# The post chain of an attention and expert kernel: Newton steps, scale and shift on GpSimd, stores of the query and key parts on SyncE's queue

## The chip, the cores and the metric

The kernel runs on one core of a Trainium2 chip. The metric is the device time in microseconds of one execution. The kernel before takes 821.72 us, the median of three runs (817.86 to 822.37). Engines: PE (TensorE, matmuls), DVE (VectorE), ACT (ScalarE), POOL (GpSimd), and SP (SyncE), which here only issues DMAs. Each takes its own instructions in order, and they wait for each other by semaphores.

## The reference

Batch 4, sequence 1024, width 128, 16 heads of width 8. All in float32.

```python
mod = (silu(c) @ wmod).reshape(4, 6, 1, 128)        # sa, ca, ga, sb, cb, gb
h = layernorm(x) * (1 + ca) + sa
Q, K, V = heads(h @ Wq.T + bq), heads(h @ Wk.T + bk), heads(h @ Wv.T + bv)
scores = Q @ K.T / sqrt(8) + lam * (tanh(Q) @ J) @ tanh(K).T     # causal
x = x + ga * ((softmax(scores) @ V) @ Wo.T + bo)
h = layernorm(x) * (1 + cb) + sb
expert = argmax(h @ centroids.T)                    # one of 8 for each row
y = h + relu((layernorm(h) * gamma + beta) @ W1.T + b1) @ W2.T + b2  # of that expert
x = x + gb * (alpha * y + (1 - alpha) * h)          # alpha = sigmoid(h . centroid)
```

## The kernel before

The work on a batch has three parts. *Preparation*: layer norm, the projections Q, K, V and the product with J, and the split of q, tanh k, k and J's product into three bf16 parts each, which go to HBM (`q_parts`, `k_parts`) and come back as stacks for the matmuls. *Attention*: four groups of four heads, g0 to g3. *The post chain*: the attended values are divided by their denominators, projected (O0, O1), added to x, normalised, scaled and shifted (this is h), multiplied with the centroids (S), the experts are chosen and counted (C), h is normalised again, and the rows of the payload are scattered to a table sorted by expert (`by_expert`). The post chain of the last batch runs in the tail, beside the experts' matmuls on 46 tiles.

A body of the main program runs the attention of batch b, the preparation of b+1 (in g0) and the post chain of b-1. The bodies are "first" (b = 0), "middle" (b = 1 and 2, a loop) and "last" (b = 3). In a group, PE makes 48 score blocks (12 units of 4 heads); ACT takes the exponential of each, PE multiplies it with the values two units later. Between the score blocks stand "items". Most of them are chunks of raw scores for the group after ("m"), whose row maxima DVE takes out of four PSUM banks. The last chunk is followed on DVE by four short steps that split the maxima into three parts (`mparts`, lines 1640 to 1643), PE turns them (item T), DVE copies them (`mrow`), and SP sends them with four DMAs (line 431, `send_maxima`) into the stacks of the next group, which can't begin before.

A table sets where in a group the items of the post chain stand: `POST_AT` for the middle body, `POST_LAST` for the last. A number there is a place out of 33 in the group's list of items. A planner (`schedule`) then lays the list over the 48 slots of PE by costs for DVE and PE. In the kernel before it puts in the middle body `attended` at slot 4 of g2, O0 at slot 10, O1 at 14, the 15 steps of the first inverse square root (`root_x`, by Newton's method, on 128x8 values) at slots 17 to 27, `scale_h` and `shift_h` at 36 and 38, H0 and H1 (transposes of h) at 43, S at the end; g3 has `best`, the 15 steps of `root_h`, C at 20 and `place`. The last body has the same in g1 and g2.

SP issues in a fixed order (`attention` in the SP block): outputs of each half group (`store_half`, line 436), the maxima, the reciprocal denominators `r_den` (`store_reciprocals`, 480), then `load_outputs` (495, 496): NUM and DEN, which `attended` multiplies. These lie where Q and K of the next batch lay until all parts were stored. The stacks of the next batch follow (`load_group`, 414). POOL splits the four tensors (631 to 636), issues three stores after each (677), then adds the residual's bias (669), and later makes the payload (688 to 700) and scatters it (712).

## Time and profile before

| | us |
|---|---|
| median of three runs | 821.72 |
| profiled execution | 825.38 |
| span of its instructions | 823.7 |
| busy: PE | 697.3 |
| busy: DVE | 569.8 |
| busy: ACT | 499.5 |
| busy: POOL | 232.3 |

The profiled execution is one run with the hardware profiler; its span is from its first to its last instruction. Busy times are sums over the whole span and say nothing of which engine ends a wait at a given place. Work of the post chain is seen in the stretches 300.6 to 389.9 (batch 0's chain), 466 to 553 (batch 1's) and 583.4 to 662.1 (batch 2's). The attention ends at 688.6. In the rows, `arenaB` holds NUM, DEN, the product AT, h and the payload, `ln` and `stat` the small values of the norms.

### The profile page before, as it was taken

How to read it: one execution, taken by the hardware profiler on the slowest of the kernel's cores; microseconds unless marked ns; L12 is line 12 of the kernel's file. 1: busy time of each engine (PE TensorE's matmuls, PEld its weight loads, DVE VectorE, ACT ScalarE, POOL GpSimd, SP SyncE). 2: the span in 40 equal slices, each digit the busy share in tenths (PEclk: the TensorE clock that was granted, in tenths of full speed). 3: DMA queues.
4: the chain of work that ended last, by engine and by line, in shares of the span. 5: the costliest groups of instructions: out<-in, count | busy, mean ns of one | idle time of the engine just before them, and what ended most of it. 6: DMA issues, size and time to landing. Idle time of an engine off the chain costs nothing.

```text
span 823.7 us, 17084 instructions
## 1 busy us (share of the span) xinstructions
PE 697.3 (85%) x5087; PEld 349.8 (42%) x5087; DVE 569.8 (69%) x1408; ACT 499.5 (61%) x1182; POOL 232.3 (28%) x218
## 2 busy tenths in 40 slices
PE   4666899999999988898899888999989879898694
PEld 2352334334334333333333334333424225788594
DVE  6959677888757777686577776778886712587453
ACT  1440786675687754575877645667575668566482
POOL 2028039400004920203049202030001400355643
PEclk9776899999999998899999998899999989998998
DMA  8995824293261349063504480537303244432520
GB/s 225 312 178 209 138 48 117 67 184 74 49 113 33 115 116 169 3 109 108 90 24 124 108 177 2 98 108 147 121 14 117 91 158 131 129 106 87 195 61 13
DMA packets 52563, 92.04 MB, mean 112 GB/s; under 512 B 10305, under 2 KB 26205, under 8 KB 51960
## 3 DMA queue, kind: packets, MB, share of 16 engines
q1 hardware_dynamic: 43404, 70.28, 36.1%
q0 software_dynamic: 6400, 17.86, 6.9%
q10 hardware_dynamic: 2668, 2.78, 1.3%
q8 instruction: 46, 0.75, 0.4%
q14 instruction: 45, 0.37, 0.2%
HBM read 51.04 MB, written 37.90 MB: 108 GB/s over the span
## 4 chain that ended last, share of the span: by engine, by line
PE 47%; DVE 19%; issue 11%; ACT 8%; DMA 8%; SPq 3%; POOL 1%; ACTq 1%; DVEq 1%; POOLq 0%
PE PS L1173 12%; PE PS L1199 10%; PE PS L1133 10%; DVE PS L1621 5%; ACT arenaA L956 5%; PE PS L1250 4%; PE PS L1261 3%; SPq L431 3%; DVE arenaB L1296 2%; DMA arenaB<-r_den 2%; DVE block_max L1628 2%; PE PS L1203 2%; DMA arenaA<-mrow 2%; ACT arenaB L874 2%; PE PS L1082 1%
## 5 line engine op out<-in xcount | busy, mean ns | idle before, releaser
L956 ACT ACTIVATE arenaA<-PS 128x512 f32<-128x512 f32 (+3 forms) x768 | 330.8, 497 | 199.4 <-PE PS L1203 157.5
L1621 DVE CUSTOM_DVE_ANT_0 PS<-PS,mask 128x1024 f32<-128x1024 f32 (+3 forms) x256 | 261.5, 1036 | 98.7 <-PE PS L1133 91.4
L1199 PE MATMUL PS<-arenaA 99*128 99x512 bf16 (+3 forms) x768 | 223.6, 337 | 23.8 <-ACT arenaA L956 9.3
L1133 PE MATMUL PS<-arenaA 96*128 96x512 bf16 (+3 forms) x768 | 202.3, 340 | 32.6 <-DVE maxima L1621 15.6
L1199 PEld LDWEIGHTS PS<-arenaA 99*128 99x128 bf16 x768 | 72.6, 98 | 220.4 <-ACT arenaA L956 132.2
L1173 PE MATMUL PS<-arenaA,Vs 128*9 128x512 f32 (+3 forms) x1536 | 163.8, 503 | 0.0
L1628 DVE TENSOR_REDUCE block_max<-PS 128x8 f32<-128x1024 f32 (+1 forms) x96 | 100.2, 1044 | 24.4 <-PE PS L1138 23.4
L1133 PEld LDWEIGHTS PS<-arenaA 96*128 96x128 bf16 x768 | 66.7, 101 | 99.8 <-DVE maxima L1621 42.0
L1203 PE MATMUL PS<-after,identb 128*128 128x128 bf16 x512 | 107.0, 225 | 1.1 <-issue 1.1
L631 POOL TENSOR_TENSOR arenaB<-arenaB 128x1024 f32<-128x1024 f32 x12 | 25.7, 2144 | 180.1 <-ACT arenaB L810 180.0
L1005 ACT ACTIVATE arenaA<-PS,b1p 128x128 f32<-128x128 f32 x184 | 52.7, 373 | 35.2 <-PE PS L1250 35.2
L768 POOL DMA_INDIRECT out_dram<-arenaA x46 | 45.8, 996 | 92.8 <-DVE arenaA L1296 90.4
L1250 PE MATMUL PS<-arenaA 128*128 128x128 f32 x368 | 53.0, 290 | 7.4 <-DVE arenaA L1752 7.3
L1203 PEld LDWEIGHTS PS<-after,identb 128*128 128x128 bf16 x512 | 51.5, 101 | 5.5 <-issue 2.0
L688 POOL TENSOR_TENSOR arenaB<-arenaB,MB 128x1024 f32<-128x1024 f32 x3 | 7.1, 2360 | 163.1 <-DVE arenaB L1296 163.1
L1261 PE MATMUL PS<-arenaA 128*128 x368 | 50.9, 284 | 1.9 <-issue 1.9
L1250 PEld LDWEIGHTS PS<-arenaA 128*128 128x128 f32 x368 | 47.7, 203 | 10.5 <-DVE arenaA L1752 10.4
L1138 PE MATMUL PS<-identb,after 128*128 128x128 bf16 x256 | 51.2, 228 | 0.0
L1261 PEld LDWEIGHTS PS<-arenaA 128*128 128x128 f32 x368 | 46.9, 200 | 2.5 <-issue 2.4
L1173 PEld LDWEIGHTS PS<-arenaA,Vs 128*9 128x9 f32 x1536 | 23.7, 89 | 51.9 <-ACT arenaA L956 26.6
L1621 DVE DVE_READ_ACCUMULATOR2_ANT maxima<- 128x1 f32 x256 | 36.1, 141 | 0.0
L1752 DVE COPY arenaA<-PS 128x128 f32<-128x128 f32 x46 | 12.9, 282 | 33.3 <-PE PS L1241 33.1
(195 smaller groups left out, 718.3 us busy)
## 6 DMA issues: line engine op xcount, KB each, us to landing
arenaA<-k_parts SPq DMA_DIRECT2D x96, 128.0 KB, 7.7
arenaA<-by_expert SPq DMA_DIRECT2D x46, 192.5 KB, 3.6
o_raw<-OT SPq DMA_DIRECT2D x32, 256.0 KB, 2.3
arenaA<-q_parts SPq DMA_DIRECT2D x16, 384.0 KB, 4.9
q_parts<-arenaB POOLq DMA_DIRECT2D x18, 256.0 KB, 3.8
k_parts<-arenaB POOLq DMA_DIRECT2D x18, 256.0 KB, 3.8
arenaA<-in_L_ffn_W_dram SPq DMA_DIRECT2D x2, 2048.0 KB, 13.3
arenaA<-q_parts SPq DMA_DIRECT2D x16, 256.0 KB, 5.7
```

The costliest lines, as they stand in the source:

```text
L768: g.indirect_dma_start(out_rows, bass.IndirectOffsetOnAxis(ap=XSI[n % NX][:, 3 * D:3 * D + 1], axis=0), YS[:, n % U, :], None, bounds_chec ...
L956: a.activation(PT[:, u % EB, h, off:HALF], PS[:, 4 + n % SB_, off:HALF], ACT.Exp).then_inc(exp_ok, 1)
L1005: last = a.activation(HR[:, n % 3, k * P:(k + 1) * P], PS[:, 3 + n % 2, k * P:(k + 1) * P], ACT.Relu, bias=b1p[:, bass.ds(expert[n] * FC + ...
L1133: last = mm(PS[:, place + c0 // HALF, at:at + c1 - c0], SQ(g, h)[0:KROWS, t * P:(t + 1) * P], SK(g, h)[0:KROWS, c0:c1], start=(at == 0), s ...
L1138: last = mm(diag, after[:, :], identb[:, :], start=False, stop=True, skip_group_check=True)
L1173: last = mm(PS[32 * h:32 * h + VW, 7, off:HALF], Vs[:, g, (kb * HG + h) * VW:(kb * HG + h + 1) * VW], PT[:, u % EB, h, off:HALF], start=(k ...
L1199: last = mm(bank[:, off:HALF], SK(g, h)[0:MROWS, kb * P:(kb + 1) * P], SQ(g, h)[0:MROWS, qc * HALF + off:(qc + 1) * HALF], start=True, sto ...
L1203: last = mm(bank[:, off:off + P], identb[:, :], after[:, :], start=False, stop=True, skip_group_check=True)
L1250: last = mm(PS[:, 3 + n % 2, k * P:(k + 1) * P], W1C[n % 3][:, k * P:(k + 1) * P], XT[:, n % 3, :], start=(k == 0), stop=True, skip_group_ ...
L1261: last = mm(PS[:, 6 + n % 2, 0:D], HR[:, n % 3, k * P:(k + 1) * P], W2T[:, bass.ds(expert[n] * FF + k * P, P)], start=(k == 0), stop=(k == ...
L1621: v.tensor_tensor_reduce(out=src, in0=src, in1=mask[:, S - n:S], scale=1.0, scalar=-3e38, op0=ALU.add, op1=ALU.max, accum_out=maxima[:, pl ...
L1628: v.tensor_reduce(block_max[:, place % 2, heads[0]:heads[-1] + 1, t, 0:t + 1], src.rearrange("p h (c q) -> p h c q", q=P), AX.X, ALU.max). ...
```

## The change

The post chain starts one group earlier: in the middle body `attended`, O0, O1 and the statistics of x stand in g1, H0, H1, S and the choice of the expert in g2, C and the places in g3. In the last body `attended` to the statistics of x stand in g0, with the reciprocals moved there from place 18 to 12, and the rest in g1 and g2. By the planner's list, in the middle body `attended` is at slot 24 of g1, O0 at 30, O1 at 33, the second half of the statistics at 37, H0 at slot 27 of g2, H1 at 28, S at 33, C at slot 4 of g3. In the last body the reciprocals are at slot 18 of g0 and `attended` at 35.

The steps of both inverse square roots for batches 0 to 2 go from DVE to POOL (`pool_moment`, 22 instructions in 18 steps that wait for each other), as do scale and shift. ACT's norms wait for them at fixed units (`NORMS_AT`). The first guess of the root takes one instruction fewer, and so has every chain 14 steps on DVE, in the tail too.

POOL no longer issues the stores of the parts. It adds the residual's bias first and then makes the four splits. SP issues the stores (`store_parts`) at four places of its order, and loads NUM and DEN between the third and the fourth tensor, as soon as the splits of Q and K are made.

```diff
         POST = ("O0", "O1", "H0", "H1", "S", "C")
         LEAD = -1400
         NEWTON = 3
-        MOMENTS = 6 + 3 * NEWTON
-        root = lambda name, n0, at, n1=MOMENTS: tuple((at + (n - n0) // 2, "D", (name, n)) for n in range(n0, n1))
-        ATT = 4
-
+        MOMENTS, POOL_MOMENTS = 5 + 3 * NEWTON, 6 + 4 * NEWTON
         POST_AT = {0: ((24, "D", "denominators"),),
-                   2: ((ATT, "D", "attended"), (ATT + 2, "R", "O0"), (ATT + 3, "D", "stats_x0"), (ATT + 4, "R", "O1"),
-                       (ATT + 5, "D", "stats_x1")) + root("root_x", 0, ATT + 6) +
-                      ((ATT + 14, "D", "bias_x"), (ATT + 19, "D", "scale_h"), (ATT + 20, "D", "shift_h"),
-                       (ATT + 22, "R", "H0"), (ATT + 23, "R", "H1"), (ATT + 23, "D", "stats_h0"), (ATT + 25, "D", "stats_h1"), (ATT + 27, "R", "S")),
-                   3: tuple(it for n in range(6) for it in ((n, "D", ("best", n)), (n, "D", ("root_h", 2 * n)), (n, "D", ("root_h", 2 * n + 1)))) +
-                      root("root_h", 12, 6) + ((8, "D", "bias_h"), (8, "D", "weigh"), (9, "R", "C")) +
-                      tuple((11 + n, "D", ("place", n)) for n in range(3))}
-
-        POST_LAST = {0: ((18, "D", "denominators"),), 1: POST_AT[2], 2: POST_AT[3] + ((15, "D", "pads"),), 3: ((0, "D", "table"),)}
+                   1: ((17, "D", "attended"), (19, "R", "O0"), (20, "D", "stats_x0"), (21, "R", "O1"), (23, "D", "stats_x1")),
+                   2: ((18, "R", "H0"), (19, "R", "H1"), (19, "D", "stats_h0"), (20, "D", "stats_h1"), (21, "R", "S")) +
+                      tuple((23 + n, "D", ("best", n)) for n in range(6)) + ((29, "D", "weigh"),),
+                   3: ((2, "R", "C"),) + tuple((4 + n, "D", ("place", n)) for n in range(3))}
+        NORMS_AT = dict(middle=dict(x=(2, 2), h=(3, 1)), last=dict(x=(1, 2), h=(2, 1)))
+
+        POST_LAST = {0: ((12, "D", "denominators"), (24, "D", "attended"), (26, "R", "O0"), (27, "D", "stats_x0"), (28, "R", "O1"),
+                         (29, "D", "stats_x1")),
+                     1: POST_AT[2], 2: POST_AT[3] + ((9, "D", "pads"),), 3: ((0, "D", "table"),)}
...
-        BEST_IN = dict(middle=3, last=2)
+        BEST_IN = dict(middle=2, last=1)
...
+        POS0_NUM, POS0_DEN = [next(n for n, it in enumerate(TENSORS) if it[0] == k) for k in (0, 1)]
...
+            def store_parts(b, n):
+
+                k, dst, off = TENSORS[n]
+                sp.wait_ge(split_ok, b * 4 + n - 3)
+                sp.sem_inc(sp_turn, 1)
+                for j in range(3):
+                    sp.dma_start(dst[bass.ds(b, 1), :, j, off:off + HD, :].rearrange("a h r q -> (a h) r q"),
+                                 T16[:, k, j, :]).then_inc(parts_out, 16)
+
             def prepared(b):
 
-                sp.wait_ge(stored, b + 1)
-                sp.sem_inc(sp_turn, 1)
+                sp.wait_ge(parts_out, b * PARTS_OUT)
+                sp.sem_inc(stored, 1)
...
-                    sp.wait_ge(stored, b + 3)
+                    sp.wait_ge(split_ok, b * 4 + 4 + POS0_NUM + 1)
                     sp.sem_inc(sp_turn, 1)
                 if not last:
                     sp.dma_start(NUM[:, :], by_head(b)[:, 0:HD, :]).then_inc(num_in, 16)
+                if not isinstance(b, int):
+                    sp.wait_ge(split_ok, b * 4 + 4 + POS0_DEN + 1)
+                    sp.sem_inc(sp_turn, 1)
                 sp.dma_start(DEN[:, :], r_den[bass.ds(b, 1), :, :].rearrange("a h (o q) -> (a h) o q", o=1).to_broadcast([H, HD, S]))\
                     .then_inc(num_in, 16)
 
...
                 if body != "first":
                     load_denominators(b - 1)
                 for g in range(NG):
+                    if body != "last" and g == 1:
+                        store_parts(b + 1, 2)
+                        if body == "middle":
+                            load_outputs(b - 1)
+                        store_parts(b + 1, 3)
                     store_half(b, g, 0)
...
-                    if g == 1 and body == "middle":
-                        load_outputs(b - 1)
                     if body == "last" and g == 2:
                         begin(0)
+                    if body != "last" and g == 0:
+                        store_parts(b + 1, 0)
                     store_half(b, g, 1)
...
+                    if g == 0 and body != "last":
+                        store_parts(b + 1, 1)
...
             def split_batch(b):
-                for n, (k, dst, off) in enumerate(TENSORS):
+                residual(b)
+                for n in range(len(TENSORS)):
                     split(b, n, split_ok)
-                    pool.wait_ge(split_ok, b * 4 + n - 3)
+
+            L2 = lambda k: ln2[:, k, :]
+
+            def pool_moment(n):
+
+                L, y = lambda k: ln2[:, k, :], ln2[:, 7, :]
+                if n == 0:
+                    g.tensor_tensor(L(0), stat2[:, :, 1], stat2[:, :, 4], ALU.add)
+                    g.tensor_tensor(L(2), stat2[:, :, 2], stat2[:, :, 5], ALU.add)
+                    return g.tensor_tensor(L(1), stat2[:, :, 1], stat2[:, :, 4], ALU.subtract)
+                if n == 1:
+                    g.tensor_scalar(L(0), L(0), -0.5, None, ALU.mult)
+                    g.tensor_scalar(L(2), L(2), 1.0 / D, EPS, ALU.mult, ALU.add)
+                    return g.tensor_scalar(L(1), L(1), 0.5, None, ALU.mult)
+                if n == 2:
+                    return g.tensor_tensor(L(3), L(1), L(1), ALU.mult)
+                if n == 3:
+                    return g.tensor_tensor(L(5), L(3), L(2), ALU.add)
+                if n == 4:
+                    return g.tensor_scalar(y.bitcast(I32), L(5).bitcast(I32), -0.5, float(0x5f3759df), ALU.mult, ALU.add)
+                if n == POOL_MOMENTS - 1:
+                    return g.tensor_tensor(L(8), L(0), y, ALU.mult)
+                if n % 4 == 1:
+                    return g.tensor_tensor(L(6), y, y, ALU.mult)
+                if n % 4 == 2:
+                    return g.tensor_tensor(L(6), L(6), L(5), ALU.mult)
+                if n % 4 == 3:
+                    return g.tensor_scalar(L(6), L(6), -0.5, 1.5, ALU.mult, ALU.add)
+                return g.tensor_tensor(y, y, L(6), ALU.mult)
+
+            def moments(b, which, stats_ok, moments_ok):
+
+                pool.wait_ge(stats_ok, b + 1)
+                pool.sem_inc(pool_turn, 1)
+                for n in range(POOL_MOMENTS):
+                    ins = pool_moment(n)
+                    if n == POOL_MOMENTS - 1:
+                        ins.then_inc(moments_ok, 1)
+                        return
+                    ins.then_inc(moments_step, 1)
+                    pool.wait_ge(moments_step, (b * 2 + which) * (POOL_MOMENTS - 1) + n + 1)
                     pool.sem_inc(pool_turn, 1)
-                    for j in range(3):
-                        pool.dma_start(dst[bass.ds(b, 1), :, j, off:off + HD, :].rearrange("a h r q -> (a h) r q"),
-                                       T16[:, k, j, :]).then_inc(parts_out, 16)
-                residual(b)
-                pool.wait_ge(parts_out, b * PARTS_OUT)
-                pool.sem_inc(stored, 1)
+
+            def scale_shift(b):
+
+                over = lambda k: MB[:, bass.ds(b, 1), k, :].to_broadcast([P, TB, D])
+                pool.wait_ge(x_normed, b + 1)
+                pool.sem_inc(pool_turn, 1)
+                g.tensor_tensor(H2, H2, over(2), ALU.mult).then_inc(h_scaled, 1)
+                pool.wait_ge(h_scaled, b + 1)
+                pool.sem_inc(pool_turn, 1)
+                g.tensor_tensor(H2, H2, over(1), ALU.add).then_inc(h2_ok, 1)
 
             def row_sums(b):
                 over = lambda k: MB[:, bass.ds(b, 1), k, :].to_broadcast([P, TB, D])
+                pool.wait_ge(stored, min(b + 3, B) if isinstance(b, int) else b + 3)
+                pool.sem_inc(pool_turn, 1)
                 pool.wait_ge(h2_ok, b + 1)
                 pool.sem_inc(pool_turn, 1)
                 g.tensor_tensor(PAY[:, :, D:2 * D], H2, over(3), ALU.mult).then_inc(pool_step, 1)
+                moments(b, 1, h_stats, h_moments)
                 pool.wait_ge(pool_step, b * 4 + 1)
...
             def send_rows(b):
 
+                moments(b, 0, x_stats, x_moments)
+                scale_shift(b)
                 row_sums(b)
...
-            def post_norm(b, dst, src, first, count):
-
-                act.wait_ge(post_chain, b * LINKS + count)
+            def post_norm(b, dst, src, first, moments_ok):
+
+                act.wait_ge(moments_ok, b + 1)
...
-                    for name, g, which in (("bias_x", BEST_IN[body] - 1, (norm_x0, norm_x1)), ("bias_h", BEST_IN[body], (norm_h0, norm_h1))):
-                        u = unit_of(body, g, "D", name)
+                    for name, which in (("x", (norm_x0, norm_x1)), ("h", (norm_h0, norm_h1))):
+                        g, u = NORMS_AT[body][name]
                         for n, step in enumerate(which):
-                            steps.setdefault((g, min(NU - 1, u + n)), []).append((1 + n, step, -1))
+                            steps.setdefault((g, u + n), []).append((1 + n, step, -1))
...
-                    return v.tensor_scalar(L(6).bitcast(I32), L(5).bitcast(I32), 1, None, ALU.logical_shift_right)
-                if n == 5:
-                    return v.tensor_scalar(L(7).bitcast(I32), L(6).bitcast(I32), -1.0, float(0x5f3759df), ALU.mult, ALU.add)
+                    return v.tensor_scalar(L(7).bitcast(I32), L(5).bitcast(I32), -0.5, float(0x5f3759df), ALU.mult, ALU.add)
+                if n % 3 == 2:
+                    return v.scalar_tensor_tensor(L(6), L(7), -0.5, L(7), ALU.mult, ALU.mult)
                 if n % 3 == 0:
-                    return v.scalar_tensor_tensor(L(6), L(7), -0.5, L(7), ALU.mult, ALU.mult)
-                if n % 3 == 1:
                     return tt(L(6), L(6), L(5), ALU.mult)
                 return v.scalar_tensor_tensor(L(7), L(6), 1.5, L(7), ALU.add, ALU.mult)
...
-                    last.then_inc(post_chain, 1)
+                    last.then_inc(post_chain if isinstance(b, int) and b == B - 1 else done, 1)
...
-                elif step in ("bias_x", "bias_h"):
-                    linked(b, AT_NORM_X if step == "bias_x" else AT_NORM_H)
-                    v.scalar_tensor_tensor(L2(8), L2(0), -1.0, L2(7), ALU.mult, ALU.mult).then_inc(post_chain, 1)
```

The semaphores of the new steps are added too, and `row_sums` waits for the stores before it writes the payload over the parts.

DVE in the last body. The first piece is of before, in g0, where the reciprocals stand (DENP is their tile; `ISA PS,maxima` is the maximum of a chunk, `block_max` that of a chunk of several heads):

```order
L1621 ISA PS,maxima<-PS,mask 128x896
L1621 ISA maxima 128x1
L1628 TENSOR_REDUCE block_max<-PS 128x4x2
L1621 ISA PS,maxima<-PS,mask 128x1024
L1621 ISA maxima 128x1
L1621 ISA PS,maxima<-PS,mask 128x768
L1621 ISA maxima 128x1
L1621 ISA PS,maxima<-PS,mask 128x1024
L1621 ISA maxima 128x1
L1621 ISA PS,maxima<-PS,mask 128x896
L1621 ISA maxima 128x1
L1443 RECIPROCAL DENP<-DENP 128x128
```


And of the change, the same place:

```order
L1680 ISA PS,maxima<-PS,mask 128x768
L1680 ISA maxima 128x1
L1680 ISA PS,maxima<-PS,mask 128x896
L1680 ISA maxima 128x1
L1687 TENSOR_REDUCE block_max<-PS 128x2x4
L1680 ISA PS,maxima<-PS,mask 128x768
L1680 ISA maxima 128x1
L1680 ISA PS,maxima<-PS,mask 128x896
L1680 ISA maxima 128x1
L1687 TENSOR_REDUCE block_max<-PS 128x4x2
L1505 RECIPROCAL DENP<-DENP 128x128
```


The reciprocals stand four maxima of a chunk earlier, right behind a `block_max` of four heads.

SP in a middle body, from the store of `r_den` to the loads of NUM (`arenaB<-o_raw`) and DEN (`arenaB<-r_den`). Before:

```order
L480 ISA
L480 DMA r_den<-DENP 128x128
L435 ISA
L436 ISA
L436 DMA o_raw<-OT 128x512
L429 REGISTER_ALU
L431 DMA arenaA<-mrow 3x8x128 x4
L441 REGISTER_ALU
L484 REGISTER_ALU
L495 REGISTER_ALU
L495 DMA arenaB<-o_raw 128x1x1024
L496 DMA arenaB<-r_den 128x1x1024
```


With the change, `r_den` is stored behind the output of g0's second half as before, and behind it stand the stores of the second and the third tensor (six DMAs). Then:

```order
L490 REGISTER_ALU
L498 ISA
L501 REGISTER_ALU
L501 DMA arenaB<-o_raw 128x1x1024
L503 REGISTER_ALU
L505 DMA arenaB<-r_den 128x1x1024
L442 DMA q_parts<-arenaB 16x8x1024 x3
L432 ISA
L433 ISA
L433 DMA o_raw<-OT 128x512
L426 REGISTER_ALU
L428 DMA arenaA<-mrow 3x8x128 x4
```


The loads stood behind the output of g1's first half and the sends of g1's maxima; now two tensors' stores stand between `r_den` and them, and the sends behind.

## Rows read from the trace of the kernel before

**Rows 1.** Busy us by stretch (PE, PEld, DVE, ACT, POOL), PEclk, DMA share, GB/s

```profile
160.20:193.20 33.00, 30.50 (x241) 12.09 (x241) 26.95 (x61) 21.41 (x50) 0.00 (x0) 1.00 0.63 122
193.20:225.70 32.50, 31.02 (x258) 12.28 (x259) 26.22 (x64) 21.23 (x50) 0.00 (x0) 1.00 0.38 71
225.70:269.90 44.20, 39.72 (x266) 16.17 (x263) 28.46 (x53) 34.80 (x72) 11.96 (x9) 1.00 0.35 72
269.90:300.60 30.70, 30.20 (x241) 12.07 (x241) 24.28 (x44) 21.51 (x50) 21.51 (x17) 1.00 0.33 98
300.60:352.10 51.50, 41.99 (x283) 18.14 (x282) 34.82 (x88) 25.16 (x60) 4.69 (x3) 0.87 0.53 99
352.10:389.90 37.80, 32.23 (x278) 13.11 (x275) 28.36 (x76) 24.57 (x60) 9.73 (x9) 0.99 0.48 111
389.90:552.80 162.90, 144.80 (x1057) 60.71 (x1057) 116.02 (x258) 105.45 (x240) 47.97 (x37) 0.95 0.41 92
552.80:583.40 30.60, 29.34 (x230) 11.81 (x226) 24.31 (x45) 21.25 (x50) 0.00 (x0) 1.00 0.57 114
583.40:625.00 41.60, 37.59 (x281) 16.24 (x282) 34.21 (x88) 25.12 (x60) 4.71 (x3) 0.97 0.18 65
625.00:662.10 37.10, 29.21 (x240) 11.16 (x237) 26.90 (x84) 24.01 (x59) 9.63 (x9) 0.96 0.32 115
```

**Rows 2.** Lines of DVE, 300.6:352.1: busy, mean ns, idle before, releasers

```profile
L1296 DVE TENSOR_TENSOR arenaB<-arenaB,MB 128x1024 f32<-128x1024 f32 x2 | 2.5, 1225 | 2.8 <-ACT arenaB L874 2.5 <-DVE arenaB L1296 0.3
...
L1296 DVE TENSOR_TENSOR X<-X,PS 128x512 f32 x2 | 1.4, 688 | 3.4 <-PE PS L1082 3.4
L1296 DVE TENSOR_TENSOR arenaB<-arenaB 128x1024 f32<-128x1024 f32 x1 | 1.2, 1224 | 3.2 <-DMA arenaB<-r_den 3.2
```

**Rows 3.** Lines of PE in the same stretch

```profile
L1082 PE MATMUL PS<-WOG,arenaB 128*128 x16 | 3.2, 361 | 3.3 <-DVE maxima L1621 3.3
L1093 PE MATMUL PS<-cols,arenaB 128*128 128x8 f32 x16 | 2.0, 257 | 0.2 <-DVE maxima L1621 0.2
L1089 PE MATMUL PS<-ident,arenaB 128*128 128x128 f32 x8 | 1.7, 357 | 1.7 <-DVE arenaB L1296 1.6
```

**Rows 4.** Line 1642: duration ns min/median/max, first and last start

```profile
L1642 DVE CAST mparts<-mres x16: 180/181/2004, 79.7 to 656.6; 128x32 bf16<-128x32 f32 x16
```

**Rows 5.** Timeline of POOL from 256 us: start, us, instruction, idle before it

```profile
256.73 2.14 POOL L631 TENSOR_TENSOR arenaB<-arenaB 128x1024 f32<-128x1024 f32 x1 [103.50 <-ACT arenaB L810]
...
263.91 1.71 POOL L677 DMA_DIRECT2D q_parts<-arenaB  x3 [0.77 <-POOL arenaB L636]
```

**Rows 6.** Timeline of SP's DMA issues from 262 us

```profile
264.03 3.38 SPq L431 DMA_DIRECT2D arenaA<-mrow  x4
...
276.21 0.33 SPq L480 DMA_DIRECT2D r_den<-DENP  x1
...
296.29 3.00 SPq L431 DMA_DIRECT2D arenaA<-mrow  x4
...
306.68 1.37 SPq L414 DMA_DIRECT2D arenaA<-q_parts  x3
```

**Rows 7.** Line 496 (load of r_den) at 300.7 us

```profile
DMA to landing us min/median/max: 6.2/6.2/6.2
```

**Rows 8.** Timeline of DVE, in g1 of batch 1 and g0 of batch 3

```profile
284.70 1.23 DVE L1621 CUSTOM_DVE_ANT_0 PS<-PS,mask 128x1024 f32<-128x1024 f32 x1
...
562.82 1.22 DVE L1628 TENSOR_REDUCE block_max<-PS 128x8 f32<-128x1024 f32 x1
```

**Rows 9.** All instructions of lines 688 and 692 on POOL: ns min/median/max

```profile
L688 POOL TENSOR_TENSOR arenaB<-arenaB,MB x3: 2352/2357/2371, 341.9 to 616.2; 128x1024 f32<-128x1024 f32 x3
...
L692 POOL TENSOR_TENSOR arenaB<-token,iotai x3: 204/204/204, 346.6 to 620.9; 128x8 int32<-128x8 int32 x3
```

**Rows 10.** Load of the denominators (line 476) in batch 3: issue and landing

```profile
559.47 0.62 SPq L476 DMA_DIRECT2D DENP<-o_raw  x1
...
DMA to landing us min/median/max: 8.6/8.6/8.6
```

37 lines of the change are left out of this document (17 added, 20 removed).

## The prediction

> **What bounds the kernel now.** I read three views. The page's shares of busy time say only who is nearest to the bound on average (TensorE), not where time is lost. So I begin with the busy time by stretch, one stretch for each attention group [rows 1]. An attention group is four heads of one batch. A batch has four groups, here called g0 to g3, and each body of the loop runs the groups of batch b and prepares b+1 and finishes b-1 beside them. The reader is to compare the stretches with each other. A g1 of a middle body holds nothing but attention and takes 30.7 us, of which PE works 30.2. The first body's g2 and g3, with loads of the next stacks and some statistics on DVE, take 33.0 and 32.5. But the middle body's g2, which holds the start of the post chain of batch b-1, takes 51.5 us with PE busy for 42.0 and at a granted clock of 0.87, and its g3 takes 37.8. Batch 2's body is the same again (162.9 against 164.2). In the last body the chain lies in g1 and g2: 41.6 and 37.1. So where the chain is absent PE is the bound, and where it is present, something holds PE up. Then the lines of that g2, with what DVE and PE wait for in it [rows 2, 3]. DVE stands 3.2 us for the transfer of the reciprocals (r_den), 3.4 us before its two additions of the projected output, 2.5 us for the normalised rows of ACT; PE stands 3.3 us before the output projection and 1.7 before the transposes. Both take their work in order, so every such stand holds the maxima behind it, and with them the four PSUM banks that PE needs.
>
> **The change, part by part.** All terms are made against the profiled execution (span 823.7, 825.4 with what lies around it). The median of the three timed runs is 821.7, 3.7 below, and I take the same difference off it.
>
> *g0 of the middle bodies.* The attention work and the projections stay. Only the stores of the split parts leave POOL's queue for SP's, behind the sends of the maxima. The four sends took 3.38 us where POOL issued stores at the same time, and 3.00 where it did not [rows 6]. At worst nothing changes; I take the 0.4 between them. The first split still starts when ACT is ready (256.7) and still lies under DVE's split of the maxima, so that stays slow there. 44.2 becomes 43.8.
>
> *Splits without issues between them.* Before, each split cost 6.4 us and then 2.5 of waiting and issuing (256.73 to 263.14 and to 265.62 for the first, [rows 5]). After, four follow each other at 6.4: they end at about 282.4, where the delays between them made it some 289. The residual, which followed them as a pass of 2.4 us, goes in front. DVE's step on the maxima near the end of g1, just ahead of the sends at 296.3 [rows 6], is then no longer under a POOL pass. A scalar step of it takes 0.18 us in the median and 2.0 at most [rows 4]. I take half of that, 0.9, off g1, and 0.8 in the first body.
>
> *g1 gets "attended", O0, O1 and the statistics.* PE: 3.2 us for the output projection [rows 3], in a group where PE is the bound, so all of it counts. The order below the diff shows SP's queue: r_den is stored after the second half's output (276.2 [rows 6]), then SP issues six stores of parts (0.46 us each, as three of its loads take 1.37 [rows 6]) and only then the loads of NUM and DEN, at about 280.5. The landing takes 6.2 us [rows 7], so about 287, or 288.5 if the six stores in front slow it. DVE comes to "attended" after the chunk that it finished at 285.9 [rows 8]. The wait is then 1 to 2.6 us, where it was 3.2; I take 2. Two handovers from PE to DVE and back remain; they cost DVE 3.4 us before [rows 2], now with a unit between them: I take 1.5, between 0 and 3.4. So g1 is 30.7 - 0.9 + 3.2 + 2 + 1.5 = 36.5.
>
> *The Newton steps leave DVE.* On DVE some 30 short instructions per batch with a wait on each predecessor go away (88 DVE instructions in g2 against 44 in g1 [rows 1]). On POOL there are 22 small instructions in 18 linked steps for each of the two norms. The trace has no such chain on POOL. Its nearest small one takes 0.20 us [rows 9]; a register instruction and a wait between two such may cost as much again. I take 0.4 a step, 7.5 us a chain. Bounds: 4.4 us (no waits) and 18 x 1 us. The statistics of x stand at slot 37 of 48 in g1, so they end some 5 us before g2, and ACT's norm stands at the third of twelve units, some 5 us into g2. So 7.5 us fit into about 10, and cost nothing in the middle bodies; beyond 10 they hold ACT, which holds PE.
>
> *Scale and shift on POOL.* Each is a pass like the one of 2.36 us [rows 9], where DVE took 1.22 [rows 2]. ACT's norms stand in the third and fourth of twelve units, so they end about 10.4 us into g2, and the two passes with their waits at 15.4. The transposes H0 stand at slot 27 of 48. By equal slots of 30.7 us that is 17 us in; the first units are short ones, so I take 15 to 17. So the passes are just covered: 0 to 1 us of wait.
>
> *g2 then.* The bare group with loads is 33.0. H0, H1 and S are 1.7 + 2.0 us of PE [rows 3]. ACT's eight norms, the handover H to S and the cover just missed: 0 to 4.3 (1.7 and 2.5 are the waits that stood there before), I take 0.8. Together 37.5, against 51.5.
>
> *g3.* 32.5, and PE's counting matmuls, 1.2 by the difference of the busy times of two g3 (32.2 and 31.0) [rows 1]: 33.7 against 37.8. The POOL work behind it (sum, factors, scatter) starts earlier than before and is waited for by none.
>
> *Middle bodies.* 43.8 + 36.5 + 37.5 + 33.7 = 151.5 against 164.2, so -12.7. For batch 2, whose plain groups are a little longer, 152.5 against 162.9, so -10.4.
>
> *Last body.* g0 now holds all up to the statistics. The reciprocals stand there in the order right behind the chunk that DVE ended at 564.0 [rows 8]. But their input is issued at 559.47, behind ten loads of the last stack, and takes 8.6 us, to 568.1 [rows 10]. Nothing in the change makes that earlier. DVE stands for 4.1 us, and PE, two chunks later, with it: 4. With 3.2 of projection and 1 of handover, 30.6 becomes 38.8. g1: 30.7 + 3.7 + 2.1 (norms whose moments come in only 3 us before their slot, H0) = 36.5 against 41.6. g2: 33.7 against 37.1. Together 109.0 against 109.3, so -0.3. The gain of this body is eaten by the early reciprocals.
>
> *Tail.* One of 15 link steps goes from each of two chains on DVE, 0.2 us each with its wait: -0.4.
>
> Sum: -0.8 - 12.7 - 10.4 - 0.3 - 0.4 = -24.6. So 800.8 for the profiled kind, 797 as a median.
>
> A rule against the change is weighed here. The long POOL passes slow some of DVE's instructions: 0.18 us against up to 2.0 [rows 4]. The Trainium skill, GPSIMD Engine Reference, Key points, says that GpSimd shares its SBUF interfaces with VectorE and contends with instructions in a 2-port mode or with two SBUF inputs. The trace agrees for the scalar steps. By that rule the sum of the payload, a pass of about 2.1 us like those of [rows 5], which now comes near DVE's step on the maxima at the end of g2, would put back up to 1.6 in three groups: 802 instead of 797.
>
> **The rivals.** (a) *The waits move with the chain.* The handovers and the r_den wait cost in g1 and g2 what they did in g2 before: 3.2 + 3.4 + 2.5 = 9.1 us a batch, where I have 4.3 (2 + 1.5 + 0.8). That gives 14 us over three batches: 811. For it: DVE still works in order, and SP's queue has six stores ahead of the loads. Against it: NUM and DEN are loaded some 20 us earlier than before, where they stood behind the sends at 296.3. (b) *Everything is covered* (no r_den wait, no handover, norms in ACT's idle time): 12 us less in the terms above (2 x 4.3, and 3.1 in the last body): 785, and 781 if the last body's reciprocals are not waited for either. For it: ACT was busy only 25 of 51 us in g2 [rows 1]. (c) *Slower: POOL's chain becomes the path.* If a small POOL instruction with its wait costs 1 us, 22 of them exceed the 10 us of cover by 12; ACT stands in order with the exponentials behind it, PE stands, three times: 797 + 36 = 833. It decides from 18 us a chain, 0.83 us an instruction, where it has eaten 3 x 8.2. Against it: 0.20 us [rows 9]. (d) *Nothing gained:* SP's queue, now with stores that wait for the splits, lets the sends of the maxima come late. The split it waits for last ends at 282.4, the sends start at 296.3, so there are 13 us of room. With a delay of 12 in each middle g1 it would be 797 + 24 = 821.
>
> **How the numbers follow.** Forecast 797: 0.66. (a) 0.14, (b) 0.11, (c) 0.05, (d) 0.04. The range reaches from 781 to 813, which takes in the ends of the handovers and of the r_den wait. Differences under 0.5%, 4 us, can't be told from none here. Faster by more than that: 0.91. Within it: 0.04, from (d). Slower: 0.05, from (c).
>
> **What would show it.** Right: the middle g2 shrinks to 36 to 39 us with a clock near 1, g1 grows to 35 to 38; DVE waits 1 to 3 us for r_den in g1; small POOL instructions of 0.2 us; in the last g0 DVE stands about 4 us before the reciprocals. Wrong: ACT's norms wait for POOL for more than 2 us, the mean POOL step is over 0.6 us, g1 is over 40 us, or the sends of the maxima come later after the transpose than before.

## The result

The changed kernel takes 813.38 us (median of 10 runs, 810.21 to 817.82), the kernel before 822.55 beside it (10 runs, 817.86 to 825.67). The ratio is 0.9892 with a 95% interval of 0.9868 to 0.9915: 9.2 us faster, by the same statistic 16 us short of the forecast of 797. The sign was right, and the chain moved as forecast; the size was not, since one wait cost three times its term and a term counted as a gain was a loss. The profiled execution took 811.68 us, span 810.0.

The busy time by stretch, one per attention group where [rows 1] have the same (PE, PEld, DVE, ACT, POOL, then PEclk, DMA share, GB/s); the first row is g0 of the first body:

```profile
85.00:132.70 47.70, 43.74 (x261) 18.58 (x261) 30.82 (x53) 34.76 (x71) 18.80 (x10) 0.87 0.53 93
...
228.20:270.60 42.40, 39.67 (x266) 16.22 (x263) 27.82 (x53) 34.76 (x72) 13.44 (x7) 1.00 0.30 57
270.60:311.80 41.20, 35.18 (x262) 14.76 (x259) 28.32 (x56) 21.91 (x50) 17.04 (x25) 0.92 0.39 118
311.80:349.20 37.40, 34.89 (x265) 14.53 (x265) 28.52 (x61) 25.37 (x61) 16.72 (x33) 0.97 0.65 108
349.20:385.40 36.20, 32.17 (x278) 12.93 (x275) 24.59 (x50) 24.90 (x59) 7.93 (x8) 0.99 0.44 116
385.40:540.20 154.80, 140.18 (x1056) 58.86 (x1056) 109.01 (x218) 106.19 (x240) 54.89 (x71) 0.98 0.40 97
540.20:581.10 40.90, 34.20 (x245) 14.11 (x241) 27.93 (x56) 21.57 (x50) 1.42 (x8) 0.87 0.44 86
581.10:617.80 36.70, 34.92 (x270) 14.69 (x267) 28.08 (x61) 25.34 (x61) 18.74 (x43) 0.95 0.21 73
617.80:653.50 35.70, 28.59 (x236) 10.99 (x237) 23.70 (x59) 23.82 (x58) 7.80 (x8) 0.96 0.33 119
```

Beside [rows 1]: the middle g2 fell from 51.5 to 37.4, which is the forecast's 37.5. But g1 rose from 30.7 to 41.2, where 36.5 was forecast, and its clock fell from 1.00 to 0.92. The first row has no counterpart in [rows 1]; before it was:

```profile
86.20:129.80 43.60, 40.20 (x261) 17.16 (x261) 29.24 (x53) 34.55 (x71) 12.38 (x9) 0.96 0.60 106
```

So the first g0 lost 4.1 us, in a body for which 0.8 of gain stood. The last body's g0 took 40.9 for a forecast 38.8.

By body, measured against forecast, the two profiled executions differ so: first +4.5 us, batch 1 +5.7, batch 2 +2.4, last +4.2, the start and the tail -5.9. Together that is 10.9 us (811.68 for 800.8). The other 5.5 us of the 16 come from the step from profiled executions to medians: the profiled one of before lay 3.7 above its median, that of the changed kernel 1.7 below.

What DVE waits for in g1 of batch 1 (lines of DVE, 270.6 to 311.8; busy, mean ns, idle before), as [rows 2] did for the old g2:

```profile
L1362 DVE TENSOR_TENSOR X<-X,PS 128x512 f32 x2 | 1.4, 689 | 3.5 <-PE PS L1148 3.5
L1362 DVE TENSOR_TENSOR arenaB<-arenaB 128x1024 f32<-128x1024 f32 x1 | 1.2, 1224 | 4.6 <-DMA arenaB<-r_den 4.6
```

And PE in the same stretch, for the first row of [rows 3]:

```profile
L1148 PE MATMUL PS<-WOG,arenaB 128*128 x16 | 3.2, 361 | 4.1 <-DVE maxima L1680 4.1
```

The wait for the reciprocals is 4.6 us, where 2 was taken (1 to 2.6). Why is in the timeline of SP's issues (start, us):

```profile
276.32 0.38 SPq L433 DMA_DIRECT2D o_raw<-OT  x1
276.89 0.34 SPq L486 DMA_DIRECT2D r_den<-DENP  x1
277.56 4.78 SPq L442 DMA_DIRECT2D k_parts<-arenaB  x6
282.89 0.63 SPq L501 DMA_DIRECT2D arenaB<-o_raw  x1
283.78 0.58 SPq L505 DMA_DIRECT2D arenaB<-r_den  x1
```

r_den leaves 0.7 us later than in [rows 6], as this g1 begins 0.7 later (270.6 for 269.9). Then six stores take 4.78 us, 0.80 each and not 0.46, and the load goes out at 283.78 and not 280.5. It lands some 6.9 us later, at 290.7; over all four such loads, against the 6.2 of [rows 7]:

```profile
DMA to landing us min/median/max: 4.9/6.4/6.9
```

DVE came when it was expected, after the chunk at 285.9 [rows 8], and stood (timeline of DVE):

```profile
284.76 1.23 DVE L1680 CUSTOM_DVE_ANT_0 PS<-PS,mask 128x1024 f32<-128x1024 f32 x1
285.91 0.14 DVE L1680 DVE_READ_ACCUMULATOR2_ANT maxima<- 128x1 f32 x1
290.67 1.22 DVE L1362 TENSOR_TENSOR arenaB<-arenaB 128x1024 f32<-128x1024 f32 x1 [4.62 <-DMA arenaB<-r_den]
```

Stretches of 3 us around this stand, columns as above:

```profile
285.50:288.50 3.00, 2.80 (x17) 0.85 (x17) 0.55 (x2) 2.69 (x6) 0.00 (x0) 1.00 1.01 264
288.50:291.50 3.00, 0.51 (x3) 0.01 (x1) 0.83 (x1) 1.36 (x3) 0.00 (x0) 1.00 1.00 352
291.50:294.50 3.00, 1.39 (x6) 1.40 (x7) 2.65 (x5) 0.00 (x0) 0.00 (x0) 0.59 0.09 35
294.50:297.50 3.00, 3.00 (x15) 0.84 (x13) 1.88 (x6) 0.60 (x1) 0.00 (x0) 0.50 0.00 0
297.50:300.50 3.00, 3.00 (x19) 1.67 (x16) 0.87 (x3) 1.08 (x2) 0.00 (x0) 0.77 0.00 0
```

PE works 0.51 and 1.39 of 3 us, and behind it the granted clock is 0.50, the lower of its two levels (1.2 GHz), until about 299. PE is busy for 35.2 us in this group instead of the 33.4 of the sum (30.2 + 3.2). So a stand of 4.6 costs more than 4.6: the forecast had priced every wait at its own length.

The 3.5 us before the additions of the projected output, in the lines of DVE above, are as long as the 3.4 of [rows 2], where 1.5 was taken. They belong to the same stand: the projection waits 4.1 us for the maxima behind `attended` and then runs at the lower clock (361 ns a matmul, 278 in d1 below). With the wait for r_den gone, 0.5 us of the 3.5 is left.

In g0 of the first body, the steps on the maxima parts, which [rows 4] show at 0.18 us in the median (timeline of DVE):

```profile
118.40 1.52 DVE L1699 TENSOR_SCALAR mparts<-maxima 128x32 bf16<-128x32 f32 x1
119.96 0.19 DVE L1700 SCALAR_TENSOR_TENSOR mres<-maxima,mparts 128x32 f32<-128x32 f32 x1
120.19 2.01 DVE L1701 CAST mparts<-mres 128x32 bf16<-128x32 f32 x1
122.23 2.06 DVE L1362 TENSOR_TENSOR mparts<-mres,mparts 128x32 bf16<-128x32 f32 x1
```

POOL at that time; [rows 5] had three passes and then issues:

```profile
119.97 2.19 POOL L652 TENSOR_TENSOR arenaB<-arenaB 128x1024 bf16<-128x1024 f32 x1
122.12 2.12 POOL L647 TENSOR_TENSOR arenaB<-arenaB 128x1024 f32<-128x1024 f32 x1
124.31 1.89 POOL L650 TENSOR_TENSOR arenaB<-arenaB,zero 128x1024 bf16<-128x1024 f32 x1
```

The steps of 1.5 and 2.0 us were there before (1.54 and 2.00); that of 2.06 us is new. Before, it took 0.19 us, and POOL had no pass between 122.71 and 125.35, where it waited and issued (timelines of DVE and of POOL before):

```profile
122.79 0.19 DVE L1296 TENSOR_TENSOR mparts<-mres,mparts 128x32 bf16<-128x32 f32 x1
...
123.47 1.87 POOL L677 DMA_DIRECT2D q_parts<-arenaB  x3 [0.75 <-POOL arenaB L636]
```

Now POOL's next pass begins at 122.12 and the step ends when that pass does, at 124.3. The step is 1.9 us longer and the group 4.1. The stretches behind it tell why, of the kernel before and then of the changed one:

```profile
122.00:125.00 3.00, 2.15 (x15) 1.04 (x13) 2.48 (x6) 1.57 (x4) 2.25 (x4) 1.00 0.07 15
125.00:128.00 3.00, 3.00 (x30) 1.32 (x26) 2.25 (x4) 1.80 (x7) 2.91 (x3) 1.00 0.82 229
```

```profile
122.00:125.00 3.00, 0.79 (x2) 0.00 (x0) 2.96 (x5) 1.01 (x3) 2.92 (x3) 0.96 0.00 0
125.00:128.00 3.00, 2.65 (x15) 1.44 (x19) 2.04 (x7) 0.45 (x2) 2.92 (x2) 0.50 0.02 3
```

PE works 0.79 of 3 us instead of 2.15, and the lower clock follows it here too, until 131 us.

In the last body, the reciprocals whose input [rows 10] bring late:

```profile
555.92 0.95 DVE L1505 RECIPROCAL DENP<-DENP 128x128 f32<-128x128 f32 x1 [4.71 <-DMA DENP<-o_raw]
```

The parts of the forecast on POOL hold; first and last step of a Newton chain, and scale and shift, for [rows 9]:

```profile
305.73 0.21 POOL L698 TENSOR_TENSOR ln<-stat 128x8 f32<-128x8 f32 x1 [21.31 <-DVE stat L1492]
...
313.23 0.20 POOL L712 TENSOR_TENSOR ln<-ln 128x8 f32<-128x8 f32 x1 [0.18 <-POOL ln L719]
...
322.46 2.36 POOL L739 TENSOR_TENSOR arenaB<-arenaB,MB 128x1024 f32<-128x1024 f32 x1 [9.03 <-ACT arenaB L940]
325.08 2.36 POOL L742 TENSOR_TENSOR arenaB<-arenaB,MB 128x1024 f32<-128x1024 f32 x1 [0.26 <-POOL arenaB L739]
```

7.7 us a chain for 7.5 forecast; ACT does not wait for it. The second pass of scale and shift ends 15.6 us into g2, forecast 15.4.

### The profile page after: what moved, and what is told of

Its sections match the earlier page's. It is cut to its first block, busy times and chain, and to the rows that moved or that the text cites. A ratio compares the mean times of both kernels' runs of the same rounds, so it can differ in the third digit from the quotient of the medians.

```text
span 810.0 us, 17135 instructions
## 1 busy us (share of the span) xinstructions
PE 689.7 (85%) x5087; PEld 342.4 (42%) x5087; DVE 552.2 (68%) x1283; ACT 501.1 (62%) x1182; POOL 253.9 (31%) x320
## 4 chain that ended last, share of the span: by engine, by line
PE 52%; DVE 18%; issue 9%; ACT 8%; DMA 7%; SPq 4%; ACTq 1%; DVEq 1%; POOL 0%; POOLq 0%
PE PS L1239 13%; PE PS L1265 13%; PE PS L1199 11%; DVE PS L1680 4%; ACT arenaA L1022 4%; PE PS L1316 4%; PE PS L1327 3%; DVE block_max L1687 2%; PE PS L1269 2%; DVE arenaA L1362 2%; DMA arenaA<-mrow 2%; SPq L428 2%; ACT arenaB L940 2%; DVE arenaB L1362 2%; DMA arenaB<-r_den 2%
## 5 line engine op out<-in xcount | busy, mean ns | idle before, releaser
L1265 PE MATMUL PS<-arenaA 99*128 99x512 bf16 (+3 forms) x768 | 227.0, 339 | 22.3 <-ACT arenaA L1022 9.3
L1199 PE MATMUL PS<-arenaA 96*128 96x512 bf16 (+3 forms) x768 | 204.5, 343 | 32.2 <-DVE maxima L1680 12.6
L1071 ACT ACTIVATE arenaA<-PS,b1p 128x128 f32<-128x128 f32 x184 | 52.5, 372 | 30.7 <-PE PS L1316 30.6
L1316 PE MATMUL PS<-arenaA 128*128 128x128 f32 x368 | 51.1, 283 | 8.3 <-DVE arenaA L1811 7.0
L685 POOL TENSOR_TENSOR X<-X,ga_bo 128x1024 f32<-128x1024 f32 (+1 forms) x4 | 9.4, 2346 | 143.3 <-ACT arenaB L907 143.1
L1316 PEld LDWEIGHTS PS<-arenaA 128*128 128x128 f32 x368 | 45.3, 194 | 12.4 <-DVE arenaA L1811 12.4
L1327 PEld LDWEIGHTS PS<-arenaA 128*128 128x128 f32 x368 | 45.5, 195 | 2.4 <-issue 2.3
L776 POOL DMA_INDIRECT by_expert<-arenaB,slot x24 | 23.5, 980 | 40.7 <-ACT arenaB L940 34.3
L1680 DVE DVE_READ_ACCUMULATOR2_ANT maxima<- 128x1 f32 x256 | 36.2, 142 | 0.0
```

The lines of the kernel that those rows point to most:

```text
L1071: last = a.activation(HR[:, n % 3, k * P:(k + 1) * P], PS[:, 3 + n % 2, k * P:(k + 1) * P], ACT.Relu, bias=b1p[:, bass.ds(expert[n] * FC + ...
L1199: last = mm(PS[:, place + c0 // HALF, at:at + c1 - c0], SQ(g, h)[0:KROWS, t * P:(t + 1) * P], SK(g, h)[0:KROWS, c0:c1], start=(at == 0), s ...
L1265: last = mm(bank[:, off:HALF], SK(g, h)[0:MROWS, kb * P:(kb + 1) * P], SQ(g, h)[0:MROWS, qc * HALF + off:(qc + 1) * HALF], start=True, sto ...
L1316: last = mm(PS[:, 3 + n % 2, k * P:(k + 1) * P], W1C[n % 3][:, k * P:(k + 1) * P], XT[:, n % 3, :], start=(k == 0), stop=True, skip_group_ ...
L1327: last = mm(PS[:, 6 + n % 2, 0:D], HR[:, n % 3, k * P:(k + 1) * P], W2T[:, bass.ds(expert[n] * FF + k * P, P)], start=(k == 0), stop=(k == ...
L1680: v.tensor_tensor_reduce(out=src, in0=src, in1=mask[:, S - n:S], scale=1.0, scalar=-3e38, op0=ALU.add, op1=ALU.max, accum_out=maxima[:, pl ...
```

## The experiments

The theory, W, as it stood in the end: the change does what the sum says, and three costs account for the rest: the reciprocals loaded behind the stores in the middle g1, POOL's unbroken passes over DVE's small steps, and the stand before the reciprocals in the last g0. (Ahead of e1, W said more broadly that the waits had moved with the chain.) Rivals: the handovers between PE and DVE (H), the moves to POOL being worth little by themselves (P), and a transfer that the earlier chain has collide with others (C).

The runs went to four different chips (the first result's is not among them). Ratios are to the kernel before on the same chip, and times from different chips are not subtracted. On the chip of e1 to e4 the changed kernel itself was not timed, so what each of these edits is worth in time against it is not measured there. Length of each group in us, from the first score matmul of one to that of the next (bodies: first; middle, batch 1; middle, batch 2; last), each from the profiled execution (one each; the last number is to the last score matmul):

```
before          43.6 30.4 33.0 32.5 | 44.2 30.8 51.5 37.8 | 45.3 31.0 50.7 36.0 | 30.6 41.6 37.1 26.0
changed         47.7 30.4 33.0 32.1 | 42.4 41.2 37.4 36.2 | 44.7 39.8 37.2 33.2 | 40.9 36.6 35.7 25.9
e1 to e4, one chip
e1 pool_stores  44.3 30.4 33.0 32.1 | 44.4 39.1 37.1 43.8 | 45.5 38.4 37.1 40.8 | 40.0 36.8 44.9 25.9
e2 sp_stores    46.3 30.4 33.0 32.5 | 42.7 30.9 51.3 41.5 | 44.0 30.8 50.5 41.8 | 30.7 40.5 41.0 25.9
e3 loads_first  46.7 30.4 33.0 32.1 | 42.4 34.7 37.3 43.5 | 43.7 34.3 37.3 42.0 | 40.1 37.0 44.4 25.9
e4 recip_late   46.0 30.4 33.0 32.1 | 42.4 41.2 37.4 44.6 | 43.7 41.0 37.2 42.5 | 34.6 36.4 43.8 25.9
a0 to e5, one chip
a0 changed      46.6 30.4 33.0 32.1 | 42.4 39.9 37.4 44.4 | 45.3 40.8 37.1 41.7 | 38.1 36.4 43.0 26.0
c1 splits_after 42.6 30.4 33.0 32.1 | 42.4 42.3 37.4 44.4 | 43.5 41.5 37.2 42.6 | 37.9 36.7 43.0 26.0
n1 newton_DVE   46.0 30.4 33.0 32.1 | 42.4 43.1 38.9 44.5 | 43.8 43.2 39.1 43.0 | 38.8 35.8 42.7 25.9
e5 longer chain 47.5 30.4 33.0 32.1 | 42.4 41.0 36.2 43.6 | 45.2 39.5 36.3 40.4 | 39.5 43.9 43.9 25.9
b0 to best3, one chip
b0 before       44.3 30.3 33.0 32.5 | 43.9 31.0 50.2 39.1 | 48.1 30.9 51.7 35.2 | 30.6 43.1 37.1 26.0
s1 scatter_late 46.3 30.4 33.0 32.1 | 42.4 41.1 37.3 36.1 | 45.1 40.0 37.1 33.2 | 39.1 36.6 36.4 27.2
best2           42.2 30.4 33.0 32.1 | 42.4 35.0 37.3 36.0 | 44.7 34.9 37.3 33.2 | 34.4 36.7 35.7 26.0
best3           43.0 30.4 33.0 32.1 | 42.4 35.0 37.2 35.8 | 42.8 35.0 37.2 33.2 | 34.5 36.7 35.7 26.0
d0 to d3, one chip
d0 changed      46.1 30.4 33.0 32.1 | 42.4 41.1 37.4 36.2 | 44.5 39.9 37.1 33.2 | 38.4 37.1 36.7 27.2
d1 loads_first  48.0 30.4 33.0 32.1 | 42.4 34.3 37.3 36.2 | 44.9 34.3 37.1 33.2 | 38.1 36.4 35.7 26.2
d2 +splits      42.4 30.3 33.0 32.1 | 42.4 35.0 37.3 35.7 | 42.3 35.0 37.1 33.2 | 39.5 36.8 36.5 27.2
d3 +recip       42.6 30.4 33.0 32.1 | 42.4 35.0 37.4 36.5 | 44.8 34.9 37.1 33.7 | 34.6 36.8 37.4 26.2
```

**e1, POOL issues the stores again.**

```diff
-                        store_parts(b + 1, 2)      (and 0, 1, 3, on SP)
+                    pool.wait_ge(split_ok, b * 4 + n - 3)
+                    for j in range(3):
+                        pool.dma_start(dst[...], T16[:, k, j, :]).then_inc(parts_out, 16)
```

> The changed kernel, but POOL issues the stores of the parts again, after each split. Theory W (the waits moved with the chain: DVE still waits for r_den in g1 and for PE's output projection): the third split ends some 5 us later (about 283), DEN can't be loaded earlier than now (283.8), so the wait for r_den in g1 stays 3 to 6 us and the time stays within 3 us of the changed kernel's 813. Rival Q (SP's queue is what spoils it: six stores of 0.75 us ahead of the loads): the wait falls under 2 us and the time to 808 or less.

833.15 us against 839.5, ratio 0.9922 [0.9896, 0.9948]. The new step of 2.06 us is 0.19 again, and the first g0 is 44.3. On this chip the kernels that keep the stores on SP have 46.0 to 46.7 there (e2, e3, e4), so the new step costs 1.7 to 2.4 us of group. The load of r_den goes out at 279.92, and the waits for it are 0.4 and 1.8 us, where W had 3 to 6. So the new step and the long wait for r_den both come with the stores' move to SP.

The lengths of the middle g1 do not follow from that: 39.1 and 38.4, with hardly any wait, for 34.7 and 34.3 in e3. In the first of them `attended` itself is long (timeline of DVE):

```profile
286.34 3.08 DVE L1360 TENSOR_TENSOR arenaB<-arenaB 128x1024 f32<-128x1024 f32 x1 [0.37 <-DMA arenaB<-r_den]
```

It took 1.22 us in the changed kernel. Here it starts behind a POOL pass of the last split (286.21 to 288.34), and once more the granted clock falls behind it, to 0.59. In the second one `attended` has its 1.23 us; PE waits 1.9 us for the sent maxima at the start of the group, and the clock over its first 11.5 us is 0.71. How much of the 4 us each of these takes was not tested.

**e2, the kernel before with the stores on SP only** (the same edit the other way round).

> The kernel before, with nothing changed but the stores of the parts: SP issues them at the four places of its order, POOL adds the residual first and then splits. NUM and DEN are loaded where they were. Theory W: worth nothing or little, 819 to 824, since the sends of the maxima come after the splits anyway; the DVE steps on the maxima at the end of g1 lose their 1 us of contention (0.18 us each instead of 1.1). Rival Q: SP's longer queue costs, 825 or more. The first body's g0 tells whether its 47.7 us in the changed kernel (43.6 before) come from POOL's splits without pauses: then it is near 47 here too.

838.56 against 839.5, ratio 0.9994 [0.9974, 1.0014]. The step is 2.06 us here too, the first g0 46.3. Moving the stores brings nothing by itself. That includes the gain for which the prediction took 0.9 us off g1. The step on the maxima near its end, 1.08 us before, is short again (timeline of DVE):

```profile
294.00 0.18 DVE L1651 TENSOR_SCALAR mparts<-maxima 128x32 bf16<-128x32 f32 x1
```

But the two middle g1 are 30.9 and 30.8 us, for 30.8 and 31.0 before.

**e3, loads ahead of the stores.**

```diff
                     if body != "last" and g == 1:
-                        store_parts(b + 1, 2)
                         if body == "middle":
                             load_outputs(b - 1)
+                            store_parts(b + 1, 1)
+                        store_parts(b + 1, 2)
                         store_parts(b + 1, 3)
```

> The changed kernel, but in a middle body SP loads NUM and DEN before the stores of the second, third and fourth tensor. Theory W with the r_den wait as a term of its own: DEN is issued near 280 instead of 283.8, lands near 286.5, DVE's wait before attended falls from 4.6 to under 1.5 us, g1 from 41.2 and 39.8 to 37 to 38, the time by 4 to 6 us to 808 or so. Rival H (the handovers to and from PE bind and take up what is freed): the wait falls, but g1 stays above 39.5 and the time is within 2 us of the changed kernel's.

825.83, ratio 0.9831 [0.9798, 0.9863]. The waits for r_den are 0.75 and 0.41 us, the middle g1 34.7 and 34.3, shorter than the 37 to 38 expected and far from the 39.5 of H.

**e4, reciprocals of the last body at place 18.**

```diff
-        POST_LAST = {0: ((12, "D", "denominators"), ...
+        POST_LAST = {0: ((18, "D", "denominators"), ...
```

> The changed kernel, but in the last body the reciprocals stand at place 18 of g0 again instead of 12. Theory W: DVE's stand of about 4 us before them goes, g0 of the last body falls from 40.9 to about 37, the time by 3 to 4 us. Rival: the stand moves to attended, which needs r_den some 9 us after the reciprocals and is only 2.5 units later; then g0 stays at 40 to 41 and the time too.

832.8, ratio 0.9909 [0.9873, 0.9945]. The last g0 is 34.6: no wait at the reciprocals, 1.9 us at `attended` instead. It is 40.0 and 40.1 in e1 and e3 on the same chip.

**a0, the changed kernel again,** beside c1, n1 and e5.

> The changed kernel again, unaltered, on the chip of the next runs, as the one they are compared with. All theories: ratio to the kernel before near 0.989 (0.985 to 0.993), the group lengths within 1 us of those of its first profile (first group 47.7, second group of the middle bodies 41.2 and 39.8, first group of the last body 40.9), except the last group of the bodies, which differed by 6 to 8 us between the two chips for every kernel. A ratio below 0.98 would say that my -24.6 us was not far off and the first measurement was.

837.49 (12 runs) against 839.92, ratio 0.9983 [0.9949, 1.0017]: on this chip the change is worth hardly anything. The groups are as in the first profile but for g3, 44.4, 41.7 and 43.0 for 36.2, 33.2 and 35.7. See the last section.

**c1, splits after the maxima.**

```diff
             def split_batch(b):
                 residual(b)
+                pool.wait_ge(m_parts_ok, b * NG - 2)
```

> Changed kernel, but GpSimd's first part split of a batch waits until VectorE has split the maxima of the same body. Theory of contention: the steps on the maxima parts in the first group (2056, 2007 and 1758 ns for steps that take 180 to 204 ns alone) go back to about 0.2 us, the first body's first group from 47.7 to at most 44, the middle bodies' from 42.4 and 44.7 by 1 to 3 us; in all 3 to 8 us shorter than the changed kernel, ratio to it 0.990 to 0.996. Rival (the long steps are covered by TensorE's own work, the 4.1 us of the first body come from elsewhere, as from the part splits that end sooner or later): group lengths as in the changed kernel within 0.5 us. Third case: the splits come so late that the score matmuls of the next batch, or the stores, wait for them: groups one to three longer, ratio over 1.0.

834.82, 2.7 us less than a0 (0.997); the two intervals overlap, so this is not clear of noise, and under the 3 to 8 us that were expected. All sixteen CASTs take 0.18 us, and the first g0 is 42.6 instead of 46.6. The middle g0 hardly change (42.4 and 43.5 for 42.4 and 45.3), though two steps of 0.3 and 1.8 us became short there too; the g0 of batch 2 lies between 42.3 and 45.5 us in the kernels with the change whatever is done to these steps. In the first g0 all three long steps are gone, the two that stood in the kernel before as well. The later splits lengthen the r_den wait of the first middle body to 5.7 us (g1 42.3 for 39.9).

**n1, Newton chains on DVE at the new places** (`("nx", n)` from place 24 of g1 and `("nh", n)` from 21 of g2, two to a place; `moments` out of POOL).

> Changed kernel, but both Newton chains (root steps and bias) are done on VectorE, two of them to a place from place 24 of the second group and place 21 of the third; scale and shift stay on GpSimd, the part stores on SyncE. If moving the Newton steps off VectorE is what made the third group short (50.7 and 51.5 us before, 37.4 and 37.2 in the changed kernel), it is 4 to 8 us longer than in the changed kernel in each body. If it was the spreading of the chain over two groups and the scale and shift on GpSimd that did it, the third group is within 2 us of the changed kernel's, and the ratio to the changed kernel is 1.00 to 1.005.

847.0, 9.5 us more than a0 (1.011), ratio to before 1.0089 [1.0052, 1.0126]. Neither expectation is met: g2 is 1.5 and 2.0 us longer, not 4 to 8, but g1 is too, by 3.2 and 2.4, where the first chain begins. Together these four make 9.1. So P falls. That the rest of the old g2's length went by spreading the chain over two groups and by scale and shift on POOL is what is left over; neither was tested alone.

**e5, three more Newton iterations on POOL** (`POOL_MOMENTS = 6 + 4 * (NEWTON + 3)`, so each chain has 12 instructions more).

> Changed kernel, but GpSimd's Newton chains have three iterations more: 12 instructions more, at 0.20 us and 0.18 us between them 4.6 us more in each of 8 chains, 7.7 us to 12.3 us. Theory: the chain on GpSimd is covered (its readers come a group later), the group lengths change by less than 1 us, ratio to the changed kernel 0.998 to 1.004. The rival of the prediction in which the chain on GpSimd is the path gives 8 x 4.6 = 37 us more, ratio 1.04; one covered chain of the two 18 us, 1.02.

838.91, 1.4 us over a0, within its noise. The middle g2 have it all but covered (ACT waits 0.4 and 0.5 us, the groups are 36.2 and 36.3). The last body has not: g1 is 43.9 for 36.4, and there ACT waits long (timeline of ACT):

```profile
602.29 1.64 ACT L940 ACTIVATE arenaB<-X,ln 128x128 f32<-128x128 f32 x4 [3.98 <-POOL ln L712]
```

This is the mechanism of rival (c), at the place where the prediction saw only 3 us of room. Its price is 7.5 us of group for a wait of 4.0; that all groups would stay within 1 us, as expected, did not hold.

**b0, the kernel before once more.**

> The kernel before, unaltered, for its group lengths on the chip of the next runs: is the fourth group of the bodies longer there too (37.8, 36.0 and 37.1 us in the first profile)? If what lengthens it in the changed kernel on the other chips (44.4, 41.7 and 43.0 against 36.2, 33.2 and 35.7) is the same in both kernels, it is 6 to 8 us longer here; if the change makes it worse, 3 to 4 us, as where only the stores were moved (41.5, 41.8, 41.0).

827.46 (one run; 822.55 is the median of 15 beside it). This chip is of the first kind (g3 39.1, 35.2 and 37.1), so the question for the other kind stayed open.

**s1, the scatter later** (C).

```diff
                 pool.sem_inc(rows_made, 1)
+                pool.wait_ge(pv_ok, ((b + 1) * NG + 3) * NU + EB + 3)
```

> Changed kernel, but GpSimd's scatter of the rows waits until three units of the fourth group are multiplied after those that free the stacks: it starts some 20 us into the group, as before the change (20.6 and 21.3 us), and not at 10, where the loads of query and key parts run. Theory of collision: the stand of TensorE, VectorE and ScalarE together (1.2 to 2.2 us) and the half clock behind it are shorter, the fourth groups 3 to 5 us shorter than the changed kernel's on such a chip (44.4, 41.7 and 43.0), ratio to before 0.985 to 0.992 where the changed kernel had 0.998. Rival (the scatter alone makes the stand, whenever it runs, as in the last body, which loads nothing beside it): the stand moves with the scatter, group lengths within 1 us, ratio as the changed kernel's.

814.66, ratio 0.9918 [0.989, 0.9947], as the changed kernel on such chips; g3 36.1, 33.2, 36.4. The changed kernel was not timed on this chip. Here the earlier scatter costs nothing that shows. On a chip of the other kind it was not tried.

**best2, all three moves (e3, c1, e4).**

> Changed kernel with the three moves that the runs so far bear out: outputs and denominators loaded ahead of the stores of the last three part tensors in the middle bodies, the part splits held until the maxima parts are made, the reciprocals of the last body at place 18. Alone they gave ratios to before of 0.983, 0.994 and 0.991 where the changed kernel had 0.998 or (on the first chip) 0.989. If they add: second groups of the middle bodies 34.5, first group of the first body at most 43, first group of the last body 34.6; ratio to before 0.976 to 0.984. If the later splits push the stores so that the loads wait again, the second groups are 37 to 42 and the ratio is 0.985 or more.

792.61 us, ratio 0.9655 [0.9622, 0.9688], more than the 0.976 to 0.984 expected.

**best3, with the scatter later too.**

> The kernel of the run ahead of this one (three moves) with the scatter held to 20 us into the fourth group. By the theory of collision 3 to 5 us shorter in each of two or three bodies, ratio to before 0.966 to 0.976; by the rival within 0.003 of that kernel's ratio.

795.05, ratio 0.9685 [0.9652, 0.9719]: no gain from the scatter's place.

**d0 to d3, the causes taken away one by one on one chip.**

> The changed kernel, as the foot of a ladder on one chip. If the chip is of the kind of the first profile (fourth groups of 33 to 36 us), ratio to before 0.989; if it is of the other kind (42 to 44 us), 0.998.

> First rung: outputs and denominators loaded ahead of the stores of three part tensors in the middle bodies. Theory W (the wait for the reciprocals in the second group costs 6.5 and 5.5 us a body): 12 us below the changed kernel of this call, ratio of the two 0.985. By the prediction's own step (2 us a body) 4 us, ratio 0.995.

> Second rung: the first, and GpSimd's part splits held until the maxima parts are made. Theory of contention: the first body's first group 4 to 5 us shorter, the middle bodies' 0 to 2 us each: 4 to 7 us below the first rung. If the splits then delay the stores and loads again: no gain over the first rung.

> Third rung: the second, and the reciprocals of the last body at place 18 of its first group instead of 12. The stand before them (4.7 us) goes: 4 to 6 us below the second rung, of which the 4.1 us of the prediction would be about all. In all the ladder should come to 21 to 24 us on the changed kernel, ratio to before 0.965 on a chip of the first kind.

| | us | ratio to before | 95% |
|---|---|---|---|
| before | 823.13 | | |
| d0 changed | 813.34 | 0.9864 | 0.9823 to 0.9905 |
| d1 loads first | 800.97 | 0.9727 | 0.9688 to 0.9767 |
| d2 and splits later | 798.97 | 0.9713 | 0.9672 to 0.9754 |
| d3 and reciprocals late | 793.84 | 0.9641 | 0.9607 to 0.9676 |

Steps of 12.4, 2.0 and 5.1 us, together 19.5. The middle one alone is within the noise of six runs, and under the 4 to 7 expected; with c1 beside it, the gain in time from later splits is not shown, only the shorter first g0. In the profiles that group is 5.6 us shorter in d2, but the two middle g1 are 0.7 longer each, and the last body, which this edit leaves alone, 3.6 longer. The windows of the two middle g1 in d0 and then in d1:

```profile
270.20:311.30 41.10, 35.08 (x262) 14.75 (x259) 28.33 (x56) 21.92 (x50) 17.06 (x25) 0.92 0.40 118
...
429.40:469.30 39.90, 34.06 (x262) 14.55 (x258) 28.23 (x56) 21.91 (x50) 16.95 (x25) 0.96 0.40 122
```

```profile
271.00:305.30 34.30, 32.41 (x261) 13.71 (x257) 28.41 (x56) 21.92 (x51) 17.03 (x25) 1.00 0.45 142
423.70:458.00 34.30, 32.47 (x261) 13.67 (x257) 28.34 (x56) 21.94 (x51) 16.99 (x25) 1.00 0.45 142
```

With the wait gone the clock is 1.00 and PE's same work takes 2.7 and 1.6 us less. The waits were 4.6 and 4.5 us (0.2 and 0.5 in d1), the groups 6.8 and 5.6 longer.

## Why the prediction was right in sign and wrong in size

The step that failed is "*g1 gets "attended"*", in its term "I take 2" for the wait for r_den. It had two errors. The stores' issue was priced from loads (0.46 us) and took 0.80, which is 2.0 of the 3.3 us by which the load went out later than estimated; 0.7 is the later start of the group. And the wait was priced at its length, without the clock behind it. Taking it away brought 12.4 us over two bodies, where the forecast had paid 4 for it: 8.4 of the 16 missing. One of the prediction's own signs of being wrong, g1 over 40 us, held in batch 1 (41.2; 39.8 in batch 2). The bound of 2.6 on that wait was too low as well. [rows 5] show a store of parts at 0.57 us in POOL's issues (1.71 for three), so a load's price was not the nearest row; but that price would have put the bound at 3.3, still short of 4.6.

The second is the sentence "and 0.8 in the first body", counted as a gain. The forecast saw the contention and weighed it (1.6 us in three groups, 802) but at the wrong step, the end of g2, where the changed trace shows nothing of it. It came in the first g0: 4.1 us in the first pair of profiles. Over all profiles that group is 46.0 to 48.0 us with the stores on SP, 43.6 and 44.3 in the kernel before and 44.3 in e1, so the new step costs 1.7 to 4.4. (c1 against a0 has 4.0 and d1 against d2 5.6, but there the two older long steps went too.) The Trainium skill, GPSIMD Engine Reference, Key points, names instructions with two SBUF inputs among those that contend. The trace agrees, with 2.06 us for one and 0.19 without the pass. The step with two inputs at 119.96 stayed at 0.19; it began 0.01 us ahead of a pass. The other two long steps read one tile, and no row shows in which mode they ran. With the removal of POOL's issues their pauses went as well: the change took away the cover and I had counted only the passes' earlier end.

The third term, the stand in the last g0, "4", was near: 4.7 in the first profile, 2.7 to 4.4 in the others that have the reciprocals at place 12. But PE stood there as well, the clock was 0.50 until 565 us, and taking the stand away brought 5.1, with 1.9 us of another wait in its place.

What held: g2 at 37.4 and 37.2 (37.5), the last g1 at 36.6 (36.5), the Newton chain at 7.7 (7.5) and its cover, scale and shift at 2.36, the four sends in 3.03 us (3.38 before). g1 apart from the wait comes out at 30.7 - 0.9 + 3.2 + 1.5 = 34.5, and d1 has 34.3, but that is luck in part: e2 shows nothing for the 0.9, the projection takes 2.2 us at the full clock and not 3.2, and the handovers leave DVE waiting 0.5 to 0.7 us. H is thereby refused. Of the rivals, (a) came nearest in time (811). Its 3.2 and 3.4 both stood in g1 (4.6 and 3.5), but e3 and d1 show that the second hung on the first, and its wait for the norms did not come. (b), 785, was not reached even with the three causes gone: 792.6 and 793.8.

Two smaller misses: g3 of batch 1 is 36.2 and not 33.7, while that of batch 2 is 33.2. PE stands there, as the loop goes back to its start, for 2.6 us that no semaphore explains (waits of PE, 382 to 386 us: for whom, us in total, times, longest; then of the kernel before, 386 to 390.5 us):

```profile
PE PS L1265 <- issue: 2.6, 1, 2.6
...
PE PS L1199 <- issue: 2.5, 1, 2.5
```

So this stand was in the trace of before, in the same group. The forecast built g3 up from one of the first body, which has no jump back, and left it out. Among the queues at that time are instruction loads (the changed kernel; queue: packets, MB, share of 16 engines):

```profile
q14 instruction: 4, 0.03, 1.9%
q8 instruction: 1, 0.02, 1.2%
```

That PE waits for these is likely and was not tested. The last body's g2 was 35.7 for 33.7. At its end PE waits 3.7 us for the sent maxima, as it did before (3.8), while g3 of batch 2 has 1.0; the forecast had priced this g2 as a middle g3. The tail, from the last product with the values, was 128.9 us for 134.0 in the first pair of profiles, 5.1 shorter. In all others it was 129.5 to 133.4, with 130.8 for the kernel before again, so this may be scatter.

## What to carry to other kernels

When DMA issues leave an engine's queue, the pauses that they made go with them, so price what ran undisturbed in those pauses. Price an issue on the queue that takes it over by an issue of the same kind of transfer. A load that the critical path waits for goes ahead of stores that nobody waits for. And waits of 4.0 to 4.6 us on the path of the attention cost 5.6 to 7.5 here, so such a wait is worth more than its row says.

## What the hardware showed that was not expected

- The price of a stand. Wait and loss in the same group: 4.6 and 6.8 us, 4.5 and 5.6 (d0 to d1), 4.0 and 7.5 (e5). A DVE step that was 1.9 us longer lengthened the first g0 by 4.1. Each time PE stood, and the granted clock was 0.50 after it.
- SP's issue of a part store is 0.80 us here, and 0.97 in d1 (six in 5.85 us), against 0.46 for a stack load in [rows 6]. The same instruction has no fixed price.
- Chips differ by kind. Two gave 822.5 and 823.1 for the kernel before, as the first one did, and two 839.5 and 839.9. On the latter g3 is longer: 41.0 to 41.8 us where only the stores were moved, 40 to 45 with the chain moved. Where the kernel before loses its 17 us on such a chip was not profiled. In a0, while the scatter and the loads share the DMA engines, PE stands without a releaser in the trace, ACT 4.0 us for one that it gives as "remote", DVE 1.9 us for PE, and the half clock follows (stretches of a0):

```profile
346.80:361.80 15.00, 14.03 (x127) 5.96 (x123) 8.05 (x19) 11.41 (x29) 3.55 (x4) 0.98 0.46 93
361.80:364.80 3.00, 0.76 (x4) 0.11 (x2) 1.13 (x2) 0.12 (x1) 2.39 (x3) 0.97 1.05 240
364.80:373.80 9.00, 7.16 (x27) 1.41 (x28) 4.64 (x8) 4.71 (x9) 1.98 (x3) 0.50 0.55 195
```

The three g3 of a0 are 24 us longer than those of the first profile, and the ratio on such a chip is 0.998 against 0.986 to 0.989. What the engines wait for is not settled.
